# The second sum over states ahead of the router logits in TensorE's list

## The reference

```
h = layernorm(x) * (1 + ca) + sa
x = x + ga * mamba(h)            # in_proj, conv(4), silu, x_proj, softplus(dt), scan, out_proj
h = layernorm(x) * (1 + cb) + sb
x = x + gb * moe(h)              # gates from h @ Wg; 7 routed experts (top 1) and 1 shared
# scan: 512 channels x 16 states; h = exp(delta*A)*h + delta*u*B;  y = sum over states of h*C
# expert: z = h @ w1; a, b = split(z); out = gate * ((silu(b) * a) @ w2)
```

## Time and profile before

| | |
|---|---|
| median of 3 runs | 2514.27 us (2513.76 to 2518.05) |
| the profiled execution | 2508.63 us |
| its span, first to last instruction | 2506.6 us |
| granted TensorE clock, mean | 0.904 |
| PE / DVE / ACT / POOL busy | 2176.9 / 1929.8 / 1360.7 / 1955.7 us |

### The profile page before, as it was taken

How to read it: one execution, slowest core, us unless ns; L and a number is a source line. 1 busy time by engine, 2 the same in 40 slices (tenths; PEclk the granted TensorE clock), 3 DMA queues, 4 the chain that set the end, 5 groups by cost and what they waited for, 6 DMA issues and landing times. The chain is left out here.

```text
span 2506.6 us, 31126 instructions
## 1 busy us (share of the span) xinstructions
PE 2176.9 (87%) x7664; PEld 1058.5 (42%) x7665; DVE 1929.8 (77%) x2060; ACT 1360.7 (54%) x2440; POOL 1955.7 (78%) x840
## 2 busy tenths in 40 slices
PE   8769898988989898999898898989857649999997
PEld 3214343443434343434343443434323335566654
DVE  2799999999999999989999999999897162222222
ACT  3666666667575766666666667576644232222221
POOL 1999889898989898988989898989897014555553
PEclk9868989898989898988989898989878869999999
DMA  5443242424232333424242424232321062222221
GB/s 154 135 110 94 76 103 67 101 68 113 81 92 74 96 82 87 116 79 105 68 103 69 101 68 111 81 94 77 89 68 42 24 208 76 85 84 83 87 85 45
DMA packets 149401, 224.39 MB, mean 90 GB/s; under 512 B 48227, under 2 KB 85617, under 8 KB 145138
## 3 DMA queue, kind: packets, MB, share of 16 engines
q1 hardware_dynamic: 135858, 182.44, 28.0%
q0 software_dynamic: 13376, 40.12, 5.2%
HBM read 99.48 MB, written 31.47 MB: 52 GB/s over the span
## 5 line engine op out<-in xcount | busy, mean ns | idle before, releaser
L1023 POOL TENSOR_TENSOR hs<-hs,c_rep 128x2048 f32<-128x2048 f32 x256 | 1154.5, 4528 | 37.3 <-ACT state L767 37.2
L863 DVE TENSOR_TENSOR_SCAN hs<-dA,state,hs 128x512 f32<-128x512 f32 x768 | 931.1, 1264 | 21.0 <-ACT dA L747 16.7
L747 ACT ACTIVATE dA<-d_rep,a 128x512 f32<-128x512 f32 x1024 | 690.0, 686 | 427.7 <-DVE hs L863 423.2
L1016 POOL TENSOR_TENSOR hs<-u_rep,b_rep 128x2048 f32<-128x2048 f32 x96 | 435.5, 4536 | 88.9 <-PE bank L517 88.9
L850 DVE TENSOR_TENSOR hs<-u_ps,b_rep 128x2048 f32<-128x2048 f32 x160 | 360.9, 2272 | 8.0 <-issue 4.8
L488 PE MATMUL bank<-n,w1s 128*128 128x512 f32 x512 | 268.4, 661 | 68.0 <-DVE delta L831 39.2
L863 DVE TENSOR_TENSOR_SCAN hs<-dA,hs 128x512 f32<-128x512 f32 x256 | 294.0, 1202 | 19.7 <-ACT dA L747 18.6
L517 PE MATMUL bank<-hs,spread 128*32 128x512 f32 x2048 | 280.3, 696 | 32.1 <-POOL hs L1023 28.0
L1408 DVE TENSOR_TENSOR hid<-z,sg 128x512 f32<-128x512 f32 x70 | 48.4, 692 | 298.1 <-ACT sg L1386 298.1
L1326 PE MATMUL z<-w1r,hT 128*128 x560 | 260.5, 608 | 3.4 <-issue 2.4
L446 PE MATMUL bank<-xin,w_in 128*128 128x512 f32 x512 | 245.1, 619 | 9.2 <-ACT xin L600 9.2
(11 more groups left out here) (173 smaller groups left out, 2531.9 us busy)
## 6 DMA issues: line engine op xcount, KB each, us to landing
d_rep<-delta SPq DMA_DIRECT2D x1024, 64.0 KB, 2.0
u_rep<-us SPq DMA_DIRECT2D x384, 64.0 KB, 2.0
b_rep<-bc_rows SPq DMA_DIRECT2D x64, 256.0 KB, 4.7
c_rep<-bc_rows SPq DMA_DIRECT2D x64, 256.0 KB, 7.8
xres<-in_x SPq DMA_DIRECT2D x16, 512.0 KB, 3.6
token_rows<-xpad SPq DMA_DIRECT2D x32, 256.0 KB, 2.3
token_rows<-xres SPq DMA_DIRECT2D x16, 512.0 KB, 3.0
xin<-in_x SPq DMA_DIRECT2D x15, 512.0 KB, 9.5
```

The source lines that it names most:

```text
L747: nc.scalar.activation(dA[:, u % ABANK, :], d_rep[:, q, :], ACT.Exp, scale=t["a"][:, u:u + 1]).then_inc(da_ready, 1)
L863: nc.vector.tensor_tensor_scan(hs[:, s % RING, g, :], dA[:, u % ABANK, :], hs[:, s % RING, g, :], state[:, u:u + 1] if m else 0.0, ALU.mul ...
L1016: nc.gpsimd.tensor_tensor(hs[:, s % RING], u_rep[:, i % UBUF, :].unsqueeze(1).to_broadcast([P, NG, T]), b_rep[:, par, :].rearrange("p (g t ...
L1023: nc.gpsimd.tensor_tensor(hs[:, s % RING, :, :], hs[:, s % RING, :, :], c_rep[:, par, :].rearrange("p (g t) -> p g t", g=NG), ALU.mult).th ...
```

## The change

Two tables are edited. In `plan`, SUM 1 moves from behind GL and RB 1 to ahead of them in set 9. In `evict`, the ACT copies of GL and RB 1 move from behind set 10's first exponential to behind its third, the copy of B 0 from its third to its fourth, and that of B 1 from set 10's fourth to set 11's second. Nothing is added or removed, and `vector`, `gps` and the transfers stay.

```diff
         plan = {
-            9: [(('GL', 0), -1), (('RB', 1), -1), (('SUM', 1), 0), (('B', 0), -1), (('B', 1), -1), (('B', 2), -1), (('DB', 0), 1), (('B', 3), -1), (('DT', 2), 1)],
+            9: [(('SUM', 1), 0), (('GL', 0), -1), (('RB', 1), -1), (('B', 0), -1), (('B', 1), -1), (('B', 2), -1), (('DB', 0), 1), (('B', 3), -1), (('DT', 2), 1)],
         evict = {
-            10: [[(('GL', 0), -1), (('L0', 0), 1), (('RB', 1), -1)], [], [(('B', 0), -1)], [(('B', 1), -1)]],
-            11: [[], [], [], [(('B', 2), -1)]],
+            10: [[(('L0', 0), 1)], [], [(('GL', 0), -1), (('RB', 1), -1)], [(('B', 0), -1)]],
+            11: [[], [(('B', 1), -1)], [], [(('B', 2), -1)]],
```

## The result

| | before | after |
|---|---|---|
| median of the timed runs | 2514.02 us (2513.11 to 2518.05) | 2483.86 us (2481.83 to 2485.11) |
| profiled execution | 2508.63 us | 2485.11 us |
| its span | 2506.6 us | 2483.1 us |
| granted clock, mean | 0.904 | 0.907 |
| one of the full chunks, mean of 13 | 117.1 us | 115.5 us |

The ratio is 0.9876 (95% interval 0.9859 to 0.9893): 30 us, 1.2% faster. The time is inside the range on record, and the direction is right, but the gain is twice the 14 us that were forecast.

What follows compares the result with a forecast made beforehand. The prediction took PE's list from SUM 1 to B 3, then ACT's SRS lump, to bind; 14 chunks at about -1.0 us (half of them with a clock relapse) gave -14 us, from 2514.3 to 2500, range 2480 to 2517.

Steps and rivals of the forecast that it cites:

- SUM 1 starts at PE's arrival: On PE in set 9: SUM 1 starts within 0.2 us of PE's arrival, 4.4 us sooner than before.
- DVE's and POOL's gains at SUM 1 are mostly not kept: DVE saves 3.77 us and POOL about 4.5 at SUM 1, then both wait at sets 12 and 11 for ACT.
- three of the signs: Wait before set 12's third scan 2.5 us or more; POOL's at set 11 3 or more; POOL's for SUM under 20.
- PE's list up to B 3 sets the pace, and gains only by the clock: SUM 1 to B 3, then ACT's SRS lump, binds; GL and RB 1 at high clock bring B 0 1.84 us sooner.
- A relapse of the clock in half of the chunks: Clock falls again in GL or RB 1 in half the chunks, leaving about -1.0 us a chunk instead of -1.84.
- The bound on a relapse's price: A fall of PE's clock back to 0.50 before B 0 costs up to 1.7 us a chunk.
- SUM 2: `gate_y`'s waits for SUM 2 may shrink by up to about 10 us in all; none counted, kept for the range.
- Rival 1: The waits go for good: DVE keeps its 3.77 us a chunk, 46 us in all, time 2468; chance 8%.
- Rival 2: GL gets no faster with the clock: 0.37 us a chunk, 5 us in all, time 2509; chance 14%.
- Rivals 3 and 4: All taken back by relapses or a fixed lump, 2513, 15%; or slower, SUM 1 cold then a relapse, 2531, 13%.
- cost nothing: On ACT: copies of GL and RB 1 behind two more exponentials, 1.3 us, delay nothing, as they run during SUM 1.
- the forecast's band: About -0.4 to -1.84 us a chunk, 2486 to 2508 us, given 50%.

Runs made afterwards that it cites:

- gl_half: The changed kernel with only the first of GL's two products, 4 matmuls instead of 8 (its output differs): 2475.0 us, 0.9852 of the time before.
- db0_late: The changed kernel with DB 0 on PE behind B 3 instead of ahead of it: 2478.8 us, 0.9861 of the time before.
- gl_twice: The changed kernel with GL's eight matmuls done twice, same result: 2543.0 us, 1.0120 of the time before.
- evict_only: The kernel before with only the two rows of `evict` changed (four later ACT copies), PE's order kept: 2511.7 us, 0.9995 of the time before.
- plan_only: The kernel before with only the row of `plan` changed (SUM 1 ahead of GL and RB 1), ACT copies left: 2541.3 us, 1.0117 of the time before.
- fill3: The changed kernel with two useless dense matmuls on PE ahead of DT 1 and two ahead of SUM 1: 2474.1 us, 0.9849 of the time before.

## Why the prediction was off by half

- *SUM 1 starts at PE's arrival*: right, 0.03 us after it on average.
- *DVE's and POOL's gains at SUM 1 are mostly not kept*: right. POOL's wait for set 11's state is 2.7 us; DVE's loss splits in two, 1.2 to 1.6 us for the spread for set 12 and 0.8 to 1.2 at set 12's third scan. That the first of them would come was missed, and with it three of the signs: the wait before set 12's third scan did not grow to 2.5, POOL's at set 11 stayed under 3, and POOL's waits for SUM fell to 25.6 us and not under 20. The last goes with SUM 1's length: 5.78 us on average where 5.16 were assumed for each.
- *PE's list up to B 3 sets the pace, and gains only by the clock*: right for this change. GL and RB 1 gained 2.18 us (forecast 1.90), SUM 1 lost 0.40 (5.38 to 5.78 on average). B 0 is 1.75 us sooner, the lump 1.90, and a chunk is 1.64 us shorter. Below the change's length the pace follows PE's list only in part (gl_half, db0_late).
- *A relapse of the clock in half of the chunks*: this is the step that failed, by its size. It happened in 0 of 15 chunks. The term was -(1.84 + 0.1)/2 = -1.0 us a chunk; with no relapse it is -1.84, and 14 times that is 26 us, beside 23.5 between the first pair of profiles and 30 between the second, and 30 and 27 between the medians. The argument was that thin work does not raise the clock; what the rows did not show is how much thin work brings it down. gl_twice shows that about twice the amount does, in two chunks of three. The bound on a relapse's price was too low as well where the clock falls in GL: 3.3 us instead of 1.7.
- *SUM 2*: six waits, 9.3 us in all, in before, eleven, 6.5 us in all, in the change. Nothing was counted and 3 us came.
- Rival 1 (waits gone for good): wrong by the waits named above. Rival 2 (weight loads with a fixed price): wrong, GL's 16 loads took 1.81 us at a clock of 1.00 against 3.43 at 0.50. Rivals 3 and 4 rest on the relapse, which did not come, or on a lump that stays, and it came 1.90 us sooner.
- Of the ACT copies "cost nothing" was right as they were placed (evict_only: 0.9995); plan_only shows what the other placing costs.
- Two slips in the working, without weight: the lower end of the forecast's band, at -1.84 us a chunk, is 2488 and not 2486, and 1073.27 - 3.77 is 1069.5 and not 1069.4.

Open is why fill3, gl_half and db0_late shorten a full chunk by only about half of what PE's list gains. DVE's scans are last at `gate_y` 1 in fill3, but its idle time is still 4.2 us a chunk, and no kernel here isolates it.

## What to carry to other kernels

Where TensorE's list sets the pace, the order of a dense group and a thin one (small matmuls, bound by their weight loads) inside a stretch of low clock is worth the thin group's weight loads at the high clock, if the thin group is short: put the dense one first. Here the clock never fell with 2.3 us of thin work, and with 4.1 us and more in two chunks of three. Before counting on a faster engine, look at who arrives at the same point at the same time; here POOL did, and filling one of PE's two waits alone left SUM 1 cold and gained next to nothing; filling both gained 10 to 12 us. And when an item moves in one engine's list, move the copies that answer to it: the same change with the copies left in place turned 30 us of gain into 28 of loss.

## What the runs showed of the hardware

- A weight load of 128 columns follows the clock: GL's 16 pairs of load and matmul, with loads back to back, took 3.43 us at 0.50 and 1.81 at 1.00.
- Transposes do too (four in 1.03 and in 0.47 us).
- In plan_only the granted clock was 0.50 for 19 us in which PE was busy for 17.99. It had stood 2.64 us just before them and stood 0.74 within them, and its matmuls there were of 65 and 32 rows, then of 128. A PE that looks busy may still be at the low clock; which of these kept it there, the runs do not separate.
- 2.3 us of thin work at the high clock (GL and RB 1) was followed by no fall in 15 chunks (after). With GL done twice, 4.1 us and more, the clock fell in it or just behind it in 10 of 15 (gl_twice).
